# A two-layer sequence kernel: fp32 products of norms, cell and values each replaced by three fp32r products, level values moved, running sums in two products

## What is computed

```python
xn = _layernorm(x)
x = x + _L0_attn_ref(xn, ...) + _L0_ffn_ref(xn, ...)
xn = _layernorm(x)
x = x + _L1_attn_ref(xn, ...) + _L1_ffn_ref(xn, ...)
# L0_attn: a gated scan over the tokens
xi, z = split(xn @ W_in);  proj = xi @ W_xp
h_t = a_t * h_{t-1} + (B * xi)_t;  y = (C * h + D * xi) * silu(z) @ W_out
# L0_ffn: each token goes to one of 8 experts (argmax of xn @ Wg.T), gelu between W1 and W2
# L1_attn: 16 heads; scores times a decay and times a level weight
cg = cumsum(g);  decay = exp(cg_t - cg_s) for s <= t
W = scores * decay * Lam[level(t xor s)];  Y = W @ V;  layernorm(Y @ Wout.T + x)
# L1_ffn: a gated cell that runs over the 16 sequences
f = sigmoid(x @ wf.T + c @ uf.T + bf);  i = sigmoid(...);  g = tanh(...);  c = f * c + i * g
h = tanh(x @ wo.T + c_final @ uo.T + bo)
```

## Time and profile before

| | |
|---|---|
| three executions, us | 1040.69, 1040.73, 1041.49 |
| the profiled execution, us | 1043.34 |
| its span, first to last instruction, us | 1041.6 |
| one repeat of the loop, us | 61.50 |
| busy: TensorE, VectorE, ScalarE, GpSimd | 96%, 84%, 68%, 16% |
| mean granted TensorE clock | 0.989 of 2.4 GHz |

### The profile page before, as it was taken

How to read it: one execution, slowest core, us unless ns; L and a number is a source line. 1 busy time by engine, 2 the same in 40 slices (tenths; PEclk the granted TensorE clock), 3 DMA queues, 4 the chain that set the end, 5 groups by cost and what they waited for, 6 DMA issues and landing times. The chain is left out here.

```text
span 1041.6 us, 20102 instructions
## 1 busy us (share of the span) xinstructions
PE 1005.0 (96%) x6700; PEld 677.3 (65%) x6700; DVE 878.1 (84%) x2122; ACT 705.0 (68%) x1525; POOL 162.3 (16%) x172
## 2 busy tenths in 40 slices
PE   6899999999999999999999999999999999999984
PEld 3666757667675766757576675766667576676753
DVE  5888797979979798897979889797987979799786
ACT  4584865939577593957849396694948659395692
POOL 0020011111011111101111110111110011110176
PEclk9899999999999999999999999999999999999996
DMA  4000000000000000000000000000000000000526
GB/s 155 11 11 1 22 1 31 0 20 10 0 30 0 30 0 20 10 0 30 0 20 10 12 19 0 30 0 20 10 8 23 0 30 0 20 10 0 192 81 193
DMA packets 31908, 27.62 MB, mean 27 GB/s; under 512 B 1552, under 2 KB 25744, under 8 KB 31760
## 3 DMA queue, kind: packets, MB, share of 16 engines
q1 hardware_dynamic: 31888, 27.37, 8.1%
HBM read 15.57 MB, written 11.80 MB: 26 GB/s over the span
## 5 line engine op out<-in xcount | busy, mean ns | idle before, releaser
L1014 ACT ACTIVATE gx<-p 128x512 f32<-128x512 f32 x256 | 145.7, 596 | 11.7 <-PE p L553 7.0
L1830 POOL TENSOR_TENSOR vp<-vdw,e 128x256 f32<-128x256 f32 (+3 forms) x80 | 60.8, 790 | 442.8 <-ACT e L1063 442.8
L551 PE MATMUL p<-x1Th,Gl 128*128 128x512 f32 x256 | 120.0, 469 | 0.4 <-ACT gx L1014 0.4
L553 PE MATMUL p<-x1Th,Gh 128*128 128x512 f32 x256 | 101.0, 395 | 0.0
L552 PE MATMUL p<-x1Tl,Gh 128*128 128x512 f32 x256 | 100.2, 391 | 0.0
L962 ACT ACTIVATE gelu<-p,bias_u 128x512 f32<-128x512 f32 x32 | 22.0, 687 | 109.6 <-PE p L494 109.6
L673 PEld LDWEIGHTS p<-vbd,pair 128*128 128x128 f32 x512 | 62.6, 193 | 40.4 <-issue 26.8
L1847 POOL TENSOR_TENSOR skip<-skip,W 128x512 f32<-128x512 f32 x15 | 19.2, 1277 | 418.6 <-DVE skip L1344 418.6
L613 PEld LDWEIGHTS p<-rs,GT 128*128 128x128 f32 x512 | 60.8, 192 | 21.4 <-ACT ms L1095 13.4
L673 PE MATMUL p<-vbd,pair 128*128 128x128 f32 x512 | 74.0, 288 | 0.0
L627 PE MATMUL p<-gx,x1T 128*32 128x512 f32 x512 | 67.8, 601 | 0.9 <-ACT gx L1014 0.8
(11 more groups left out here) (278 smaller groups left out, 2597.8 us busy)
## 6 DMA issues: line engine op xcount, KB each, us to landing
xin<-in_x SPq DMA_DIRECT2D x16, 256.0 KB, 2.9
hx_scratch<-vdw SPq DMA_DIRECT2D x15, 256.0 KB, 2.6
res_scratch<-normed SPq DMA_DIRECT2D x14, 256.0 KB, 2.1
gx<-in_weights SPq DMA_DIRECT2D x1, 1216.0 KB, 11.0
vp<-hx_scratch SPq DMA_DIRECT2D x4, 256.0 KB, 3.4
GT<-res_scratch SPq DMA_DIRECT2D x4, 256.0 KB, 3.9
out<-vp SPq DMA_DIRECT2D x4, 256.0 KB, 3.4
W<-in_weights SPq DMA_DIRECT2D x1, 746.0 KB, 12.0
```

Of the source, the lines that this page charges most:

```text
L551: pe.matmul(head_bank(h)[:, :], tile(Gl, h), x1Th[:, :], start=True, stop=False)
L553: pe.matmul(head_bank(h)[:, :], tile(Gh, h), x1Th[:, :], start=False, stop=True).then_inc(R["gx_ps"], 1)
L1014: act.activation(tile(gx, h, T), head_bank(h)[:, :], ACT.Copy).then_inc(R["gx_copied"], 1)
L1830: last = pool.tensor_tensor(view(vp[:, at:at + 128 * count], "p (s h e) -> p s h e", s=count, e=HD), spread(v.unsqueeze(1), [128, count, H ...
```

## The change

- Ten fp32 products per repeat (the eight of `project`, the two of `gate_u`) and the three with the cell are made as `heads` is: three fp32r products of high and low parts, low times high, high times low, high times high. Of `values`, the 336 columns are made so for the four tiles, after the four products of 96 columns. For sequence 0 the prologue keeps the fp32 products.
- GpSimd makes the parts: `split_weights` once, at the end of the prologue (five copies and five subtractions of 256 to 512 columns), and `split_inputs`, `split_rows`, `split_cell` in every repeat, each an element-wide operation, a copy and a subtraction of 512 columns. `split_inputs` also waits for `g_ready`, `split_rows` for `h1_ready`, `split_cell` for `lam_ps`.
- `level_values` also waits for `nodes_ready` and counts `vp_ready` tile by tile; `left_halves` waits by tile.
- `running_sums` has one product with `ones` of 48 columns in place of three; VectorE prepares its input with two additions of 16 columns behind `g_ready`.
- `node_vectors` goes to the end of VectorE's prologue. In the last part the cell goes ahead of `lam_sum`, `level_weights` ahead of `node_lams`; the last turn, projection, norm and output are made in halves; VectorE has 8 of the closing additions (7 before) and GpSimd 8 (9 before), in another order, with another order of stores.
- Several tensors share memory (`x1P` with `lv`, `lev` with `alpha`, `cgt` with `lvs`, the parts with the inputs they outlive), with waits to match: `xn` and `xh` are written only after `z1_ps`, `nodesT` after `g_ps`, `lev` after `lev_ready`.

```diff
+        Winh = sb("Winh", 2 * INNER, fp32r)
+        with nc.sbuf_tensor("held2", [128, T], fp32) as held2:
+            pass
+        MBCh = sb("MBCh", 2 * INNER, fp32r)
+        W1h = sb("W1h", E * HID, fp32r)
+        Wvh = sb("Wvh", 336, fp32r)
+        gates_ch = sb("gates_ch", 3 * D, fp32r)
...
-        x1P = sb("x1P", T)
+        x1P = lv[:, 0:T]
...
-        POOL_ADDS = 9
-        spare = sb("spare", 2 * T)
+        END_DVE = (0, 1, 2, 3, 4, 5, 6, 15)
+        END_POOL = tuple(range(7, 15))
+        END_SUMS = END_DVE + END_POOL
+        END_TANH = (0, 1, 2, 7, 8, 9, 3, 10, 11, 4, 12, 13, 14, 5, 6, 15)
...
             def project(j, bank, free, value, lhs, done):
+                whole, high, low = lhs
                 pe.wait_ge(R[free], value)
-                pe.matmul(P0[bank][:, :], lhs, xnT[:, :], start=True, stop=True).then_inc(R[done], 1)
+                if not later(j):
+                    pe.matmul(P0[bank][:, :], whole, xnT[:, :], start=True, stop=True).then_inc(R[done], 1)
+                    return
+                pe.matmul(P0[bank][:, :], low, xnTh[:, :], start=True, stop=False)
+                pe.matmul(P0[bank][:, :], high, xnTl[:, :], start=False, stop=False)
+                pe.matmul(P0[bank][:, :], high, xnTh[:, :], start=False, stop=True).then_inc(R[done], 1)
...
             def scan_x(j):
-                project(j, 1, "xhT_ready", j + 1, w("Win", 0, 128), "xi0_ps")
-                project(j, 2, "top1_steps", 7 * j + 1, w("Win", 128, 256), "xi1_ps")
+                if later(j):
+                    pe.wait_ge(R["wsplit_steps"], 10)
+                    pe.wait_ge(R["xsplit_ready"], 2 * j)
+                project(j, 1, "xhT_ready", j + 1, in_part(0), "xi0_ps")
+                project(j, 2, "top1_steps", 7 * j + 1, in_part(1), "xi1_ps")
...
+                    pe.wait_ge(R["hsplit_ready"], 2 * j)
+                    pe.matmul(P0[q][:, :], tile(W1l, q), xhTh[:, :], start=True, stop=False)
+                    pe.matmul(P0[q][:, :], tile(W1h, q), xhTl[:, :], start=False, stop=False)
+                    pe.matmul(P0[q][:, :], tile(W1h, q), xhTh[:, :], start=False, stop=False)
...
+            def values_in_parts(j):
+
+                pe.wait_ge(R["x1P_ready"], j + 1)
+                for n, free in enumerate(("dlam_ready", "ym_ready", "yt_ready", "x1Th_ready")):
+                    pe.wait_ge(R[free], j + 1 if n == 3 else 4 * j)
+                    pe.matmul(P1[(2 + n) % 5][:, 336:VDW], tile(x1P, n), w("Wvdw", 336, VDW), start=True, stop=True)
+                pe.wait_ge(R["wsplit_steps"], 10)
+                for n in range(TILES):
+                    bank = P1[(2 + n) % 5]
+                    pe.matmul(bank[:, 0:336], tile(x1Th, n), Wvl[:, :], start=True, stop=False)
+                    pe.matmul(bank[:, 0:336], tile(x1Th, n), Wvh[:, :], start=False, stop=False)
+                pe.wait_ge(R["x1Tl_ready"], j + 1)
+                for n in range(TILES):
+                    pe.matmul(P1[(2 + n) % 5][:, 0:336], tile(x1Tl, n), Wvh[:, :], start=False, stop=True)\
+                        .then_inc(R["vdw_ps"], 1)
...
-                for n in range(1, TILES):
-                    mm = pe.matmul(P1[2][:, H * n:64], spread(ones[:, 0:1], [128, 128]), g[:, 0:64 - H * n],
-                                   start=False, stop=(n == TILES - 1))
-                mm.then_inc(R["cgT_ps"], 1)
+                pe.wait_ge(R["gsum_steps"], 2 * i + 2)
+                sums = view(dts[:, 576:768], "p (n c) -> p n c", c=64)[:, :, 0:H]
+                pe.matmul(P1[2][:, H:64], spread(ones[:, 0:1], [128, 128]), sums, start=False, stop=True)\
+                    .then_inc(R["cgT_ps"], 1)
...
-                pe.wait_ge(R["vp_ready"], i + 1)
                 low, high, at = slice(0, 64), slice(64, 128), (0, 512, 896, 1280)
                 pe.wait_ge(R["gx_copied"], 16 * i + 15)
                 for n in range(TILES):
 
+                    pe.wait_ge(R["vp_ready"], TILES * i + n + 1)
...
+            def recur_cell(i, n):
+
+                pe.wait_ge(R["csplit_ready"], 2 * i + 2)
+                pe.matmul(P0[n][:, :], tile(gates_cl, n), cellh[:, :], start=False, stop=False)
+                pe.matmul(P0[n][:, :], tile(gates_ch, n), celll[:, :], start=False, stop=False)
+                pe.matmul(P0[n][:, :], tile(gates_ch, n), cellh[:, :], start=False, stop=True)\
+                    .then_inc(R[("f_ps", "i_ps", "g_ps")[n]], 1)
...
                 left_ends(i)
                 recurrence(i, None, 2)
-                heads(i, 4, 13)
+                recur_cell(i, 2)
+                heads(i, 4, H)
                 cell_out()
-                heads(i, 13, H)
                 pair_scores(i, 0)
                 left_halves(i)
                 pair_levels(i, 0)
                 node_matrices(i)
-                for n in range(TILES):
-                    if n < 3:
-                        pair_scores(i, n + 1)
-                        chunk_values(i, n)
-                        levels(i, n)
-                    else:
-                        levels(i, n)
-                        chunk_values(i, n)
+                for n in range(3):
+                    pair_scores(i, n + 1)
+                    chunk_values(i, n)
+                    levels(i, n)
                     chunk_sums(i, n)
-                turn_out(i)
-                project_out(i)
+                last_turn(0, P1[2])
+                levels(i, 3)
+                chunk_values(i, 3)
+                last_project(0, P0[2])
+                chunk_sums(i, 3)
+                last_turn(1, P1[1])
+                last_project(1, P1[2])
...
+                dve.wait_ge(R["g_ready"], i + 1)
+                first = lambda n: dts[:, 576 + 64 * n:576 + 64 * n + H]
+                dve.tensor_tensor(first(1), first(0), c(9)[:, H:2 * H], ALU.add).then_inc(R["gsum_steps"], 1)
+                dve.wait_ge(R["gsum_steps"], 2 * i + 1)
+                dve.tensor_tensor(first(2), first(1), c(9)[:, 2 * H:3 * H], ALU.add).then_inc(R["gsum_steps"], 1)
...
                 token_rows(i)
                 pair_differences(i)
+                recurrence(i)
+                dve.wait_ge(R["c_ready"], B)
                 lam_sum(i)
                 fold_own(i)
-                recurrence(i)
-                dve.wait_ge(R["c_ready"], B)
+                level_weights(i)
                 node_lams(i)
+                cell_out()
                 node_rows(i)
-                cell_out()
                 pair_lams(i, 0)
                 pair_weights(i, 0)
                 for n in range(1, TILES):
                     pair_lams(i, n)
-                level_weights(i)
-                own_heads(i, 0)
-                pair_weights(i, 1)
-                level_sum(i, 0)
-                tile_sum(i, 0)
-                own_heads(i, 1)
-                pair_weights(i, 2)
-                level_sum(i, 1)
-                tile_sum(i, 1)
-                end_add(POOL_ADDS)
-                own_heads(i, 2)
-                pair_weights(i, 3)
-                level_sum(i, 2)
-                tile_sum(i, 2)
-                end_add(POOL_ADDS + 1)
-                level_sum(i, 3)
+                end_add(0)
+                for n in range(3):
+                    own_heads(i, n)
+                    pair_weights(i, n + 1)
+                    level_sum(i, n)
+                    if n == 2:
+                        end_add(3)
+                    tile_sum(i, n)
+                    end_add((1, 2, 4)[n])
+                level_products(i, 3)
                 own_heads(i, 3)
-                end_add(POOL_ADDS + 2)
+                level_total(i, 3)
+                last_attention_out(0)
                 tile_sum(i, 3)
-                for b in range(POOL_ADDS + 3, B):
+                last_stats(0)
+                for b in (5, 6, B - 1):
                     end_add(b)
-                last_attention_out()
-                stats2(i)
-                last_norm()
+                last_attention_out(1)
+                last_stats(1)
+                last_norm(0)
+                last_out(0)
+                last_norm(1)
+                last_out(1)
...
+                pool.wait_ge(R["nodes_ready"], i + 1)
...
-                last.then_inc(R["vp_ready"], 1)
+                    last.then_inc(R["vp_ready"], 1)
+
+            def split_inputs(j):
+
+                pool.wait_ge(R["xhT_ps"], j + 1)
+                pool.wait_ge(R["xnT_ready"], j + 1)
+                pool.wait_ge(R["g_ready"], j)
+                pool.tensor_tensor(xnTl[:, 0:1], xnT[:, 0:1], xnT[:, 0:1], ALU.subtract)
+                pool.wait_ge(R["wsplit_steps"], 10)
+                pool.tensor_copy(xnTh[:, :], xnT[:, :]).then_inc(R["xsplit_ready"], 1)
+                pool.wait_ge(R["xsplit_ready"], 2 * j - 1)
+                pool.tensor_tensor(xnTl[:, :], xnT[:, :], xnTh[:, :], ALU.subtract).then_inc(R["xsplit_ready"], 1)
+
+            def split_rows(i, j):
+
+                pool.wait_ge(R["h1_ready"], j + 1)
```

(63 more changed lines are left out.)

213 lines of the change are left out of this document (138 added, 75 removed).

## The result

The changed kernel takes 1022.26 us (median; 1021.82 to 1023.54) against 1040.71 in the same measurement: a ratio of 0.982, 95% interval [0.980, 0.983]. Forecast was 1010 with a range of 998 to 1027 and a likeliest part of 1002 to 1018, so faster was right, by 18 us where 31 were forecast, and the time lies in the range but above its likeliest part. Its profiled execution has a span of 1020.5 us, 21.1 less than before.

What follows compares the result with a forecast made beforehand. TensorE's order was taken to set the pace, with little room at its meetings with other engines. Per repeat -1.9 us, times 15 -28.5, prologue +2, last part -4.5: -31 us, forecast 1010 us, range 998 to 1027.

Steps and rivals of the forecast that it cites:

- Values, 0: `values` in each repeat: a quarter fewer column costs, 0.6 us, gains nothing because ScalarE's copy and VectorE's chain to `g_ready` decide.
- Recurrence, -0.2: Cell products per repeat: the first two end where `turn_x1` waits for `xn1_ready`, worth 0.05; the third counts, 0.17 us.
- Running sums, -0.1: Behind `g_ready`: two products fewer, two VectorE additions more, -0.1 us per repeat; ends -0.2 and +0.4 if a GpSimd copy holds one.
- The second rival: GpSimd's splits hold VectorE at the second running sum, +0.4 us per repeat in place of -0.1; 1020 us, chance 0.20.
- Four tiles, -0.68: gate_z and gate_u: four shorter products save 0.68 us per repeat, just fitting the 0.71 slack against `levels` of the last tile.
- scan_x, scan_b, scan_c, -0.97: Projections ahead of and among the heads: -0.8 us per repeat for scan_x, scan_b, scan_c(0), and -0.17 for scan_c(1).
- level values, 0: Level values moved behind `nodes_ready`: no gain or loss, VectorE's relief making up for the later start; ends 0 and +2.0 us.
- The splits, 0: GpSimd's three splits per repeat, some 2.0 us each, cost nothing, under VectorE work with a PSUM operand and wanted 2 us later.
- Prologue, +2: Before the loop: `node_vectors` moved back brings layer 1 forward 1.5 us, but `split_weights` may hold VectorE; +2 us, ends -3 and +6.
- Last part, -4.5: After the loop: `level_weights` moved ahead, halves and one GpSimd addition fewer save 4.5 us; ends 0 and -7.
- GpSimd's splits hold VectorE: Rival placed at the second running sum, held by a copy: 1.4 us gained per repeat, prologue +5, 1020 us; chance 0.20.
- Slower: Rival: level values come late since `node_lams` gives nothing back and `nodes_ready` stays near 504.3; +0.45 per repeat, 1047 us; chance 0.10.

Runs made afterwards that it cites:

- the three mends: Changed kernel with the cast of `split_inputs` behind the second running sum, the residual made early and four of five weight pairs split early: 1007.42 us, ratio 0.9677.

## Why the prediction was right in sign and two thirds too large

Steady repeat, forecast -1.9 us, measured -1.04. Two terms failed, the running sums and the four tiles:

*Values, 0*: right (0.00). *Recurrence, -0.2*: right (0.16); x1Th now waits 0.48 us for its products, 0.66 before, and the first two gates gave nothing, since the turned x1 waits 0.68 us for xn1.

*Running sums, -0.1*: wrong, +0.17. The step that failed is "VectorE issues its second addition about as early as GpSimd gets through its first tiny operation". GpSimd's tiny operation ended at 484.79 by its record, but the cast behind it started at 484.73, 0.03 us ahead of the addition. The second rival had the place and the mechanism, with a size of +0.4 that was too large. Among its signs of being wrong the prediction had named this one, a second running sum at 0.6 us or more. The Trainium skill, "SBUF — State Buffer", section "Who interferes with whom", says that one of the two is kept out for a whole instruction, whichever came second. By that rule a 16-column addition beside a cast of 0.61 us waits for nearly all of it. The trace agrees: 0.60 us for 0.17 alone.

*Four tiles, -0.68*: wrong, 0. This is the larger miss. The slack of 0.71 was read against `levels` of the last tile only; the other thing that ends the stretch, GpSimd's chain to `res_init`, was left out, though in the profile of before it ended 0.12 us ahead of x1's start. With the chain out of the way the stretch is 20.91 us (503.55 to 524.46), 0.47 of the 0.68. The other 0.2 is lost at the first tile, where `chunk_sums` waits for VectorE's `own_heads`; before, and with the residual early:

```profile
519.48 0.43 PE L681 MATMUL p<-ym,K 128*32 128x128 f32 x8 [0.20 <-DVE ym L1613]
```

```profile
509.29 0.43 PE L756 MATMUL p<-ym,K 128*32 128x128 f32 x8 [0.31 <-DVE ym L1750]
```

Both lie 5.74 us behind the pair lams (513.74 and 503.55), so the first product of `gate_z`, which stands ahead of them, gains nothing, and three products are left, 0.5 us. The wait of 0.20 was in the profile of before and isn't in the prediction.

*scan_x, scan_b, scan_c, -0.97; level values, 0*: their sum was nearly right (-0.85 from `g_ready` to the last pair lams, with the +0.17 of the running sums in it), the parts weren't. The prediction asked of the level values only whether TensorE's left halves would wait. They don't: the values start at 496.80, take 3.45 and so end 16.0 us behind `g_ready` (484.29), as worked out (506.0 - 490.11 = 15.9). It didn't ask whether VectorE could follow TensorE's 0.9 us. (The scores of tile 0 came 0.69 us nearer to `g_ready`: 498.11 - 484.29 for 504.62 - 490.11; the running sums took the rest.) It could not have, in the old place of the level values; the two edits earn one gain between them. That the forecast of their sum came out is in that part luck.

*The splits, 0*: right but for the one cast. Together, -1.9 + 0.27 + 0.68 is -0.95, against -1.04.

Prologue, +2: measured +3.0. x1 is 1.5 us nearer to the first `expert_b` product, as said (8.4 to 6.9), but `node_vectors`, which made room for it, now stands between x1 and the first `g_ready`. That stretch is 4.5 us longer, 1.5 of them moved and 3.0 new, beside the ten operations of `split_weights`: the four normalising operations alone take 3.04 us for 1.11. In the run with the norms' products whole, which splits neither Win nor MBC, the time from the `expert_b` product to `g_ready` is 25.8 us, so nearly all of the 3.0 is the splitting's. TensorE idles 5.50 us, and the granted clock is 0.58 in the stretch from 53 to 60 us, most of it at the lower of the two levels (1.2 GHz). With the three mends, where that wait is 0.68 us, it is 1.00 there, and 0.66 from 43 to 53 us, as before the change.

Last part, -4.5 with an end at -7: measured -7.2. `level_weights` has come out from under GpSimd's sums: its four operations took 4.5 us in the last part before (1008.13 to 1012.62), and take at most 0.28 each now. That is some 3.7 us of the 7.2; how much of the rest is the halves' was not tried.

The rival "GpSimd's splits hold VectorE" gave 1020 and the kernel took 1022, but that is a coincidence of sums: it had the running sums' place right, at +0.4 for 0.17, the prologue at +5 for +3, and the tiles' -0.68 still in it. "Slower", 1047, needed node vectors that gain nothing; they gained 1.8 us, the node rows starting 12.4 us behind `g_ready` and not 14.2 (504.31 - 490.11).

## What to carry to other kernels

A stretch ends where the last of several chains ends, and the profile prints only the last one; before booking a shorter product, list every semaphore that the next instruction waits for, and read when each was given. An edit that frees one engine can be worthless alone and worth all of it with a second edit that frees the other: try both halves of such a pair before you say which one works. And when work is put on GpSimd, start it behind the instruction of VectorE that reads SBUF twice, not behind the one before: here one semaphore's number was worth 0.29 us a repeat, over 4 us in all.

## What the hardware showed beyond that

The holding goes both ways. Beside VectorE's scan (2.37 us for two halves, as without company) GpSimd's operation on one column took 1.11 us, for 0.2 elsewhere, and its copy of 511 columns 1.59, for 0.61 for 512. Whichever starts later is the one that waits: in the first repeat with the residual early, one scan took 2.22 us behind a GpSimd addition that had itself waited for the scan ahead (2.19 for 1.29). Operations of VectorE with one tensor as input, in SBUF, are also held, as the four normalising ones (3.04 us for 1.11): with the weights split early, a copy of 144 columns (L1389) takes 1.35 us beside GpSimd's subtraction, against 0.23 in the changed kernel, where GpSimd is idle at that time. The statistics and the transposes of VectorE took the same time with and without GpSimd: four statistics 0.86 us beside a subtraction (501.85, residual early) and 0.87 elsewhere, the transpose of the node vectors 2.31 us beside the level values (496.67) and 2.31 in the kernel before.
